# Writing out the engine loops of the context attention, the latent heads and the last experts in a Perceiver stack kernel

## What is computed

```python
q_r = jnp.einsum('bshq,hqr->bhsr', q_big, W_qr)
k_r = jnp.einsum('bld,hdr->bhlr', kv_r, W_kr)
scores = jnp.einsum('bhsr,bhlr->bhsl', q_r, k_r)
attn = jax.nn.softmax(scores, axis=-1)
ctx_c = jnp.einsum('bhsl,bld->bhsd', attn, kv_r)
ctx_lat = jnp.einsum('bhsd,hkd->bhsk', ctx_c, w_kc_kv)
return ctx.transpose(0, 2, 1, 3).reshape(Bv, Sv, H * K) @ Wo.T
```

## Time and profile before

| | |
|---|---|
| median of 3 runs | 1365.63 us (1365.62 to 1365.66) |
| the profiled execution's own time | 1364.51 us |
| its span, first to last instruction | 1362.7 us |
| mean granted TensorE clock | 0.992 |
| TensorE matmul busy | 1321.3 us (97%) |
| TensorE weight load busy | 1085.0 us (80%) |
| VectorE busy | 938.6 us (69%) |
| ScalarE busy | 624.0 us (46%) |
| GpSimd busy | 661.1 us (49%) |

### The profile page before, as it was taken

The page is one execution under the profiler, slowest core; times in us unless marked ns, Lnnn a source line. Parts: engine busy times, 40 slices in busy tenths (PEclk is TensorE's granted clock), DMA queues, the critical chain, the costliest instruction groups (busy, mean ns, idle before and its releaser), DMA issues.

```text
span 1362.7 us, 22745 instructions
## 1 busy us (share of the span) xinstructions
PE 1321.3 (97%) x8567; PEld 1085.0 (80%) x8567; DVE 938.6 (69%) x1427; ACT 624.0 (46%) x1293; POOL 661.1 (49%) x478
## 2 busy tenths in 40 slices
PE   8999999999999998999999899999999999999998
PEld 5777778778875665999899899999878888767886
DVE  5556766659658996877677687877446777565555
ACT  3524443253333335666566566666324546631000
POOL 3342577768736867044043141400464656635663
PEclk9999999999999999999999899999999999999999
DMA  4121223323342220000000001000231222212321
GB/s 151 49 78 49 62 83 95 88 76 93 93 167 72 71 61 26 26 1 27 1 26 26 2 26 38 20 1 1 74 111 47 79 78 64 92 47 85 99 94 62
DMA packets 31187, 83.20 MB, mean 61 GB/s; under 512 B 3440, under 2 KB 5616, under 8 KB 30704
## 3 DMA queue, kind: packets, MB, share of 16 engines
q1 hardware_dynamic: 31088, 81.81, 19.3%
HBM read 80.75 MB, written 1.05 MB: 60 GB/s over the span
## 4 chain that ended last, share of the span: by engine, by line
PE 89%; DVE 4%; ACT 3%; issue 2%; POOL 1%; DMA 0%; ACTq 0%; POOLq 0%; DVEq 0%
PE psum L925 24%; PE psum L927 23%; PE psum L926 23%; PE psum L1477 6%; PE psum L953 1%; PE psum L1411 1%; PE psum L995 1%; PE psum L1424 1%; PE psum L1000 1%; PE psum L996 1%; PE psum L1373 1%; PE psum L964 1%; PE psum L1680 1%; DVE xc L2264 1%; PE psum L1654 1%
## 5 line engine op out<-in xcount | busy, mean ns | idle before, releaser
L671 POOL TENSOR_SCALAR wpair<-landing 128x1024 fp32r<-128x1024 f32 (+3 forms) x115 | 104.2, 906 | 369.8 <-PE psum L927 212.0
L674 POOL TENSOR_TENSOR wpair<-landing,wpair 128x1024 fp32r<-128x1024 f32 (+3 forms) x115 | 220.5, 1917 | 9.6
L925 PE MATMUL psum<-xn,wpair 128*128 128x512 f32 x548 | 222.8, 407 | 0.4 <-POOL wpair L674 0.4
L926 PE MATMUL psum<-xn,wpair 128*128 128x512 f32 x548 | 216.2, 395 | 0.0
L927 PE MATMUL psum<-xn,wpair 128*128 128x512 f32 x548 | 215.9, 394 | 0.0
L2257 DVE TENSOR_TENSOR expo_t<-psum,expo_t 128x512 fp32r<-128x512 f32 (+1 forms) x224 | 144.1, 650 | 76.1 <-ACT expo_t L2040 72.7
L2040 ACT CAST expo_t<-psum 128x512 fp32r<-128x512 f32 (+1 forms) x224 | 124.2, 565 | 130.3 <-PE psum L1477 130.3
L925 PE MATMUL psum<-expo_t,kv_pair 128*128 128x256 f32 (+1 forms) x416 | 134.1, 322 | 0.2 <-DVE expo_t L2257 0.2
L2685 DVE TENSOR_REDUCE part_max<-psum 128x1 f32<-128x804 f32 x126 | 120.5, 986 | 12.2 <-PE psum L927 10.1
L1477 PE MATMUL psum<-const,expo 128*128 128x128 f32 (+1 forms) x832 | 127.4, 273 | 0.9 <-DVE expo_t L2257 0.6
L925 PEld LDWEIGHTS psum<-xn,wpair 128*128 128x128 f32 x548 | 103.3, 188 | 30.8 <-issue 7.0
(11 more groups left out here) (324 smaller groups left out, 3058.7 us busy)
## 6 DMA issues: line engine op xcount, KB each, us to landing
landing<-in_weights SPq DMA_DIRECT2D x60, 512.0 KB, 3.5
landing<-in_weights SPq DMA_DIRECT2D x103, 256.0 KB, 2.6
kv<-in_ctx SPq DMA_DIRECT2D x8, 832.0 KB, 4.8
landing<-in_weights SPq DMA_DIRECT2D x15, 320.0 KB, 2.8
landing<-in_weights SPq DMA_DIRECT2D x16, 192.0 KB, 2.3
rotary_w<-in_rotary SPq DMA_DIRECT2D x1, 1920.0 KB, 10.0
rope_k<-in_rope_k SPq DMA_DIRECT2D x1, 1664.0 KB, 13.9
const<-in_constants SPq DMA_DIRECT2D x1, 1184.0 KB, 8.6
```

Source lines behind the costliest of these rows:

```text
L671: pool.tensor_scalar(wpair[:, slot, 0, 0:width], landing[:, slot, 0:width], 1.0, 1.0, ALU.mult, ALU.mult).then_inc(chunk_high, 1)
L674: pool.tensor_tensor(wpair[:, slot, 1, 0:width], landing[:, slot, 0:width], wpair[:, slot, 0, 0:width].bitcast(F32), ALU.subtract).then_in ...
L925: pe.matmul(out, w(0), act(0), start=start, stop=False)
L926: pe.matmul(out, w(0), act(1), start=False, stop=False)
```

## The change

Eight loops of the kernel are written out: `Fori` becomes `range`. Nothing else is touched. The numbers in the waits and the operands stay the same; they are constants now instead of register values.

```diff
@@ gpsimd, context steps of batches 2 to 7
-                with pool.Fori(1, B // 2) as i:
+                for i in range(1, B // 2):
                     for j in range(2):
                         whole(context_steps(2 * i + j, j, True))
@@ tensor, context attention
-                with pe.Fori(0, B // 2 - 1) as i:
+                for i in range(B // 2 - 1):
                     units(i, False)
                 units(B // 2 - 1, True)
@@ tensor, latent heads
-                with pe.Fori(1, 7) as i:
+                for i in range(1, 7):
                     for j in (1, 2):
                         latent_head(2 * i + j, j)
@@ tensor, last experts
-                with pe.Fori(0, 3) as i:
+                for i in range(3):
                     for j in range(2):
                         expert_f(2 * i + j + 2, FB + 7 + 6 * i + 3 * j, (FB + 1 + j) % 2)
@@ scalar, context attention
-                with act.Fori(0, B // 2 - 1) as i:
+                for i in range(B // 2 - 1):
                     units(i, False)
@@ scalar, latent heads
-                with act.Fori(1, XH // 2 - 1) as i:
+                for i in range(1, XH // 2 - 1):
                     for j in range(2):
                         latents_in(2 * i + j, j)
                         head_context(2 * i + j + 2, j)
@@ scalar, last experts
-                with act.Fori(2, NE) as e:
+                for e in range(2, NE):
                     act.wait_ge(mid_step, 4 * (2 * NE + e))
                     silus_f(e)
@@ vector, latent heads
-                with dve.Fori(1, XH // 2 - 1) as i:
+                for i in range(1, XH // 2 - 1):
                     for j in range(2):
                         latents_in(2 * i + j, j)
                         head_context(2 * i + j + 2, j)
```

## The result

The changed kernel takes **1348.61 us** (median of 6 runs, 1346.02 to 1352.65). The kernel before, timed beside it, takes 1365.53 us (6 runs, 1362.48 to 1365.66). The ratio is 0.9884 [0.9865, 0.9903]. The forecast was 1353.4 us with a range of 1350.8 to 1356.8.

The account below looks back on a forecast made before the run. TensorE was taken as the bound, losing time at two context-loop back edges: 11.5 us there, 0.7 behind them, 0 elsewhere, sum 12.2 us. Off the median 1365.63 that gave 1353.4 us, range 1350.8 to 1356.8.

Parts of the forecast that it names:

- The third interval is the forecast in small: TensorE context attention, 852.95 to 865.37: same work without a jump back, 12.42 us against 18.10 and 18.25.
- The twin: Third 92-matmul context interval, falling through into the written-out copy; comparison with it prices two back edges at 11.51 us together.
- Both pieces belong to the jump: TensorE's idle 1.50 and 2.69 us at the first context back edge: the branch, then instructions that had not arrived.
- rival 2: ScalarE is the wait, as profiled: 1.50 and 1.88 us stay, gain 8.8, time 1356.8 us; 5%.
- The body is short: TensorE's latent heads and last experts: bodies of 60 and 289 instructions, no gap to win, taken as 0.
- rival 3: Stops move into the straight line through four more packets; slower from three stops on, 1377 us with all four; 3%.
- Fetching in a straight line at 0: Written-out latent heads and experts add 878 instructions, 4 packets, priced at 0; upper bound 23 us.
- 29 packets in 412 us: Context passes on TensorE already fetch as they go, so writing them out adds no packets there.
- rival 4: The stop is not the loop's but something recurring every 108 us; nothing changes, 1365.6 us; 2%.
- The sum against the profiled execution: Whole kernel: 11.5 + 0.7 + 0 + 0 = 12.2 us, against the profiled 1364.51 us giving 1352.3.
- taken off the median, the forecast is 1353.4 us: Whole kernel: the 12.2 us gain subtracted from the median before, 1365.63 us, 1.1 us above the profiled execution.
- Rival 1: Clock falls at other places, giving 1351.9 or 1354.9 us, or 1352.3; 20% for 1 us or more off, mostly low.

## Why the prediction was wrong, point by point

- **"The third interval is the forecast in small."** Right. The twin took 12.42 us, the two units take 12.29 now; 11.77 us came from them against a summed 11.51, and 0.66 us behind them against 0.71. TensorE's context loop alone gives the whole effect, all the rest none, one back edge half.
- **"Both pieces belong to the jump."** Right, and rival 2 (ScalarE, 1356.8 us) is refuted: its piece stands at 1.86 us with ScalarE's loop written out, and is gone at both units with ScalarE's loop kept. That the stops are instructions that had not arrived is shown by the packets of the shifted loop, 53 against 71.
- **"The body is short", so 0 for latent heads and experts.** The value was right, the reason not the one. The prediction put it as length, 1500 against 60 and 289. A body of 1722 instructions jumps back free, and the context body itself does when it is shifted by 80. Short bodies touch 1 or 2 pages. The "some 1500" left out the 144 other instructions; it is 1652. The measured room is 7 pages, 1792 instructions, counted from the page in which the body starts. The room of 2048 instructions in the Trainium skill ("Runtime: NRT & Kernel Launch", Instruction fetch mechanics), weighed in rival 3, is 8 such pages, one more than measured, and the section says nothing of where a body starts; by the room alone the 1652 instructions would have been free wherever they lie, and the earlier trace rows show that they were not. The same section says that a branch out of a window of two pages stalls, 512 instructions; the bodies of 1482 to 1722 instructions that jump back free on TensorE show that it is wider here.
- **"Fetching in a straight line at 0."** Right. The latent heads and the expert passes show packets beside them and TensorE busy for all of 46.00 and 33.60 us; the page counts 68 packets in place of 71. The working behind it was off. The 71 packets are not one per 241 instructions run: they are the 53 of a program that never fetches again, and 18 for the two back edges. So the "29 packets in 412 us" were in good part the stops' own, and the written-out passes fetch others in their place. Rival 3 (1377 us) did not happen, nor rival 4. The 108 ns of the Trainium skill's "Advanced Engine Details and Errata", Control Flow Timing, would give 0.2 us for the two back edges, by an estimate; the windows say 11.77.
- **The sum against the profiled execution.** 12.2 summed, 13.5 measured. Missing were the terms outside the loops' ends: 0.78 us at unit 20, 0.28 at units 4 and 24, 0.3 near 1243 us. By the traces these are waits that depend on when other engines' work falls, and the prediction had no term for them. It explains 1.3 of the 4.8 us by which the forecast missed.
- **The step that failed: "taken off the median, the forecast is 1353.4 us".** The mechanism and its size held; the level from which the sum was taken did not. It took three runs of the kernel before, 0.04 us apart, for its level, and took the clock's falls for fixed. Over 17, 12 and 7 further runs the kernel before has 1362.25, 1361.36 and 1361.39 us, within 1359.1 to 1365.45, so the level was 3.4 to 4.3 us too high; the changed kernel spreads over 6.6 us. The profiled execution before, 1364.51 us, was on the upper side too. Rival 1 named the clock, with 1.5 + 1.1 us on the low side and 20%; the term should have been about 4 us. That the clock made the first three runs slow is not shown, since their clocks are not on record. Against the larger samples the change is worth 1.0%: 0.9898 [0.9881, 0.9914], and 0.9909 [0.9889, 0.9928] for TensorE's context loop alone. The forecast's own ratio, 1353.4 / 1365.63 = 0.991, lies in both and outside [0.9865, 0.9903] of the first comparison. The gain in the first of them is 13.7 us, against 12.2 summed.

Left open: why those first runs of the kernel before agreed so closely and so high; why the wait near 412 us varies; what decides, after the same wait near 21 us, whether the clock falls. The collision at unit 20 (VectorE's 2.15 us operation beside GpSimd) was read from the traces alone and not tried.

## What to carry to other kernels

A loop on TensorE costs nothing at its back edge until its body touches one page of instructions too many (here an eighth page of 256); from there a back edge costs 2 to 6 us, and whether it does depends on where in the program the body starts. So look at the back edge in the trace ("issue", or a wait whose releaser had long been done), and compare the packets of the instruction queue with the length of the program: packets beyond it are fetched again. Before writing a long loop out try shifting or shortening it. A forecast of 1% needs the level of the kernel before over a dozen runs, not three that happen to agree, and a term for how often the clock falls.

## What the runs showed of the hardware

- **A step at 7 pages of instructions on TensorE.** Bodies of 1482, 1542, 1602 and 1722 instructions free, 1654, 1802, 2002 and 2202 not; 19 loops in all, 12 free and 7 stopped, agree with "at most 7 pages of 256", and no other page size from 32 to 1024 instructions (powers of two) fits them with any limit. Two of the 19, the shifted ones, were forecast by it.
- **The instruction queue tells whether a loop is fetched again.** 53 packets for a program of 13723 instructions whose back edges are free, 71 for 13643 whose two back edges stop; some 9 packets for each stop.
- **A back edge beyond the step stops TensorE in one piece or two.** One piece, 1.7 to 2.1 us, where 81 or more instructions of the target's page follow the jump; two, such as 1.50 + 2.69 or 1.40 + 1.61 us, where 28 or fewer do (1.74 + 2.83 us in the weight loads where one does). In the context loop two pieces, with the interval's clock at 0.84 to 0.92, cost 5.8 to 6.3 us; one piece cost 2.0 us at a clock of 1.00 and 3.2 at 0.92.
- **The profile's releaser can be an innocent one.** The first piece is put down to ScalarE at L2033 or L2034 in every run of the context loop that has it. In the kernel before the read had ended 1.9 us earlier, and with ScalarE's loop written out the piece stayed.
- **Executions of one program differ by 6.6 us in 1349** with a mean granted clock of 0.995 to 0.999, and with two idle stretches filled four runs lay within 1.7.
